# Mixture of experts: spreading the routing weights four rows at a time, and moving the residual sum to ACT and GpSimd

## The reference, cut to what matters

```python
t = t + _L1_ffn_ref(_ln_t(t), ...)          # 65536 tokens of 64 channels

def _L1_ffn_ref(x, router_w, router_b, expert_w, expert_b):
    B, N, D, C, E, K = (8, 4096, 64, 64, 8, 2)
    router_probs = jax.nn.softmax(x @ router_w + router_b, axis=-1)
    top_p, top_i = jax.lax.top_k(router_probs, K)
    top_p = top_p / jnp.sum(top_p, axis=-1, keepdims=True)
    expert_out = jnp.einsum('bnd,edc->bnec', x, expert_w) + expert_b
    gathered = jnp.take_along_axis(expert_out, top_i[..., None], axis=2)
    return jnp.einsum('bnk,bnkc->bnc', top_p, gathered)
```

## Time and profile before

| | |
|---|---|
| timed executions (three) | median 2308.48 us, 2306.16 to 2319.19 |
| profiled execution | 2298.41 us, span of the instructions 2296.6 us |
| PE / VectorE busy over the whole span | 1752.8 us (76%) / 1584.8 us (69%) |
| ACT / GpSimd busy over the whole span | 1142.8 us (50%) / 1168.2 us (51%) |
| the experts | first load of x at 1715.5 us, first spread at 1761.9, last store issued at 2292.6 |
| granted clock, mean over the span | 0.913 |

### The profile page before, as it was taken

How to read it: one execution, slowest core, us unless ns; L and a number is a source line. 1 busy time by engine, 2 the same in 40 slices (tenths; PEclk the granted TensorE clock), 3 DMA queues, 4 the chain that set the end, 5 groups by cost and what they waited for, 6 DMA issues and landing times. The chain is left out here.

```text
span 2296.6 us, 44402 instructions
## 1 busy us (share of the span) xinstructions
PE 1752.8 (76%) x11740; PEld 1164.1 (51%) x11740; DVE 1584.8 (69%) x5005; ACT 1142.8 (50%) x2610; POOL 1168.2 (51%) x1594
## 2 busy tenths in 40 slices
PE   5778748888646659838887737978746999999998
PEld 3444437778522238724444426877734444444443
DVE  6888704566757768838787730665664889889887
ACT  5898813333125549817676633333216545555541
POOL 5777604676857740026566520766765343444330
PEclk9999979999779989959999979999885999999999
DMA  3777547888633314958789746988764555555552
GB/s 115 204 193 190 156 137 240 273 297 284 209 117 93 95 51 82 191 179 242 233 252 267 217 115 179 311 276 272 260 193 144 155 157 158 155 158 160 153 140 68
DMA packets 475473, 423.19 MB, mean 184 GB/s; under 512 B 224690, under 2 KB 372402, under 8 KB 475314
## 3 DMA queue, kind: packets, MB, share of 16 engines
q1 hardware_dynamic: 402610, 303.87, 47.4%
q10 hardware_dynamic: 72704, 117.47, 15.2%
HBM read 236.68 MB, written 150.99 MB: 169 GB/s over the span
## 5 line engine op out<-in xcount | busy, mean ns | idle before, releaser
L699 PE MATMUL cp_pv<-cp_weight,cp_zt 64*128 64x320 f32 x2048 | 369.8, 469 | 103.4 <-ACT cp_zt L637 87.8
L257 POOL TENSOR_TENSOR cc_ln_rstd<-cc_ln_var,numbers 128x8 f32<-128x8 f32 x128 | 255.5, 1996 | 188.5 <-DVE cc_ln_var L248 179.6
L523 DVE SCALAR_TENSOR_TENSOR a_res<-cp_pv,cp_mask,cp_sig 128x64 f32<-128x64 f32 x1024 | 263.9, 322 | 123.9 <-ACT cp_sig L646 119.4
L1537 DVE TENSOR_TENSOR ex_xe<-ex_spread,ex_xd 128x512 f32<-128x512 f32 x512 | 322.6, 683 | 36.0 <-PE ex_spread L1779 35.8
L829 PE MATMUL cc_sum<-a_res,cc_bch 128*128 (+1 forms) x2048 | 297.9, 296 | 62.6 <-DMA cc_bch<-b_scratch 59.3
L919 ACT ACTIVATE cc_p<-cc_sum 128x512 f32 (+1 forms) x128 | 135.8, 1061 | 376.4 <-PE cc_sum L829 239.7
L829 PEld LDWEIGHTS cc_sum<-a_res,cc_bch 128*128 128x128 f32 x2048 | 269.8, 205 | 85.0 <-issue 76.1
L646 ACT ACTIVATE cp_sig<-cp_pv 128x384 f32<-128x384 f32 x512 | 249.7, 493 | 125.7 <-PE cp_pv L699 124.0
L699 PEld LDWEIGHTS cp_pv<-cp_weight,cp_zt 64*128 64x128 f32 x2048 | 184.3, 189 | 222.3 <-issue 193.7
L1796 PE MATMUL ex_po<-ex_xe,ex_expert 128*64 128x512 f32 x1024 | 267.8, 647 | 0.1
L1589 POOL TENSOR_TENSOR ex_rstd<-ex_var,numbers 128x8 f32<-128x8 f32 x64 | 104.7, 1636 | 270.4 <-DVE ex_var L1485 260.5
(11 more groups left out here) (186 smaller groups left out, 2976.4 us busy)
## 6 DMA issues: line engine op xcount, KB each, us to landing
cc_bch<-b_scratch SPq DMA_DIRECT2D x256, 256.0 KB, 3.9
gate_scratch<-cp_sig SPq DMA_DIRECT2D x128, 256.0 KB, 2.6
b_scratch<-cp_b_stage SPq DMA_DIRECT2D x128, 256.0 KB, 4.0
cc_g<-gate_scratch ACTq DMA_DIRECT2D x128, 256.0 KB, 4.5
after_conv<-cc_p ACTq DMA_DIRECT2D x128, 256.0 KB, 3.8
ex_xd<-ex_xt SPq DMA_DIRECT2D x256, 128.0 KB, 2.5
cp_x<-in_x SPq DMA_DIRECT2D x64, 256.0 KB, 3.3
cc_p<-in_x ACTq DMA_DIRECT2D x64, 256.0 KB, 3.6
```

The costliest lines, as they stand in the source:

```text
L257: pool.tensor_tensor(rstd[q][:], var[q][:], numbers[:, 0:1].to_broadcast([P, tiles]), ALU.pow).then_inc(scaled if shifts else known, 1)
L523: dve.scalar_tensor_tensor(a_res[:, h, :, row], bank[:, h, 3 * C:4 * C], mask_sb[:, h, row:row + 1], sig[u.mod(2)][:, 0, h, i, :], ALU.mul ...
L699: pe.matmul(pv[slot(u, i)][:, h, 0:COLS], zt[u.mod(2)][half, i * P:(i + 1) * P], weight[half, :], start=True, stop=True).then_inc(v_made, 1)
L1537: dve.tensor_tensor(xe[u.mod(2)][:, :, h, i * P:(i + 1) * P], pb[2 * (p % 2) + h][:].rearrange("p (e t) -> p e t", e=EP), xd[u.mod(8)][:, ...
```

## The change

- The spreads of a unit come in two groups instead of four. A group fills all four banks with 16 matmuls, of which four in a row use the four different groups of 32 rows (`FOURS`). It may start when all four blocks of the group before are done. Each bank has a semaphore of its own.
- VectorE's step: four blocks, half of the measuring, the choosing or the split, four blocks, the rest of the measuring, the choosing. Measuring is one unit further ahead.
- The sum with x leaves VectorE. ACT copies `tb` into the new tile `turned` (`take_turned`, first in its step), and GpSimd adds it to `rest` (`finish`, first in its step). The store comes a step later.
- PE's order in a step: experts half 1, flip, spread, experts half 2, rating, spread of the next unit, transposes of the output. Before: spread, flip, experts half 1, spread, experts half 2, spread, rating, spread, transposes.
- ACT normalises in two parts around `take`. The tiles of x are 8 instead of 4, those of the statistics 4 instead of 2, and the loop has one step more at each end.

The diff, cut to its core:

```diff
-        xs = [m.sb(f"x{q}", [P, H, R, C]) for q in range(4)]
+        xs = [m.sb(f"x{q}", [P, H, R, C]) for q in range(8)]
...
+        turned = [m.sb(f"turned{q}", [P, R * P]) for q in range(2)]
...
+        FOURS = [[(0, 0), (1, 1), (0, 2), (1, 3)], [(1, 0), (0, 1), (1, 2), (0, 3)]]
+        FIRST, LAST, HEAD, TAIL = -13, G + 2, 16, 16
...
 (SyncE)
-                    load(s + 12)
+                    load(s + 13)
                     double(s + 7)
-                    load_rest(s + 1)
+                    load_rest(s)
...
 (VectorE)
+                def scale_inputs(u, g, k):
+                    h, i = FOURS[g][k]
...
+                    dve.wait_ge(spread_made[k], u.n * 2 + g + 1)
                     dve.tensor_tensor(xe[u.mod(2)][:, :, h, i * P:(i + 1) * P],
-                                      pb[2 * (p % 2) + h][:].rearrange("p (e t) -> p e t", e=EP),
+                                      pb[k][:].rearrange("p (e t) -> p e t", e=EP),
...
-                    scale_inputs(s, 0, 0)
-                    scale_inputs(s, 0, 1)
-                    finish(s - 2)
-                    scale_inputs(s, 1, 0)
-                    scale_inputs(s, 1, 1)
-                    measure(s + 10)
+                    for k in range(4):
+                        scale_inputs(s, 0, k)
+                    measure(s + 11, 0)
                     if turn == 0:
                         choose(four, 0)
                     if turn == 1:
                         choose(four, 2)
                     if turn == 3:
                         split_shares(s + 1)
-                    scale_inputs(s, 2, 0)
-                    scale_inputs(s, 2, 1)
-                    scale_inputs(s, 3, 0)
-                    scale_inputs(s, 3, 1)
+                    for k in range(4):
+                        scale_inputs(s, 1, k)
+                    measure(s + 11, 1)
...
 (GpSimd)
+                def finish(u):
+                    if not u.real:
+                        return
+                    pool.wait_ge(turned_copied, u.n + 1)
+                    pool.wait_ge(rest_in[u.mod(4)], u.div(4) * 16 + 16)
+                    to = rest[u.mod(4)][:].rearrange("p h i c -> p i h c")
+                    pool.tensor_tensor(to, turned[u.mod(2)][:].rearrange("p (i h c) -> p i h c", i=R, h=H), to, ALU.add
+                                       ).then_inc(out_made, 1)
...
+                    finish(s - 2)
                     if turn == 1:
                         weigh(four, 1)
                     find_scales(s + 10)
...
 (ACT)
+                def take_turned(u):
...
+                    act.activation(turned[u.mod(2)][:], tb[:], ACT.Copy).then_inc(turned_copied, 1)
...
+                    take_turned(s - 2)
                     if turn == 3:
                         take_shares(s + 1)
+                    normalise(s + 9, 0)
                     take(s + 8)
-                    normalise(s + 9)
-                    store(s - 2)
                     if turn == 2:
                         weigh(s + 2)
+                    normalise(s + 9, 1)
                     take_outputs(s - 1)
+                    store(s - 3)
                     take_logits(s + 8)
...
 (TensorE)
-                    if p >= 2 or (u - 1).real:
-                        pe.wait_ge(xe_dve, u.n * DVE_BLOCKS + 2 * p - 2)
+                    if g or (u - 1).real:
+                        pe.wait_ge(xe_made, (2 * u.n + g) * R)
...
                     for e in range(EP):
-                        for h in range(H):
-                            q = (p + h) % R
-                            ins = pe.matmul(pb[2 * (p % 2) + h][:, e * P:(e + 1) * P],
-                                            select[32 * q:32 * q + 32, h, e, :], rows[32 * q:32 * q + 32, :],
-                                            start=True, stop=True)
+                        for k, (h, i) in enumerate(FOURS[g]):
+                            ins = pe.matmul(pb[k][:, e * P:(e + 1) * P], select[32 * i:32 * i + 32, h, e, :],
+                                            rows[32 * i:32 * i + 32, :], start=True, stop=True)
                             if e == EP - 1:
-                                ins.then_inc(spread_b if h else spread_a, 1)
+                                ins.then_inc(spread_made[k], 1)
...
-                    spread_out(s, 2)
+                    add_experts(s - 1, 0)
                     flip(s + 8)
-                    add_experts(s - 1, 0)
-                    spread_out(s, 3)
+                    spread_out(s, 1)
                     add_experts(s - 1, 1)
+                    rate(s + 8)
                     spread_out(s + 1, 0)
-                    rate(s + 8)
-                    spread_out(s + 1, 1)
                     turn_outputs(s - 1)
```

More of the change, by code:

```diff
@@ L1361, in experts @@
         yt = m.sb("yt", [P, R * P])
[L1362 to L1365 removed]
+        turned = [m.sb(f"turned{q}", [P, R * P]) for q in range(2)]
+        stats = [m.sb(f"stats{q}", [P, T, 3]) for q in range(4)]
+        var = [m.sb(f"var{q}", [P, T]) for q in range(4)]
+        rstd = [m.sb(f"rstd{q}", [P, T]) for q in range(4)]
+        lift = [m.sb(f"lift{q}", [P, T]) for q in range(4)]
         T4 = 4 * T
@@ L1406, in _ @@
                 dve.tensor_copy(router[:], pb[1][:, 0:H * E]).then_inc(weights_made, 1)
-        x_in = [m.sem(f"x_in{q}") for q in range(4)]
+        x_in = [m.sem(f"x_in{q}") for q in range(8)]
         rest_in = [m.sem(f"rest_in{q}") for q in range(4)]
```

100 lines of the change are left out of this document (46 added, 54 removed).

## The result

| | before | after |
|---|---|---|
| timed executions (four each, on one chip) | median 2307.32 us, 2304.51 to 2319.19 | median 2228.52 us, 2223.46 to 2237.77 |
| profiled execution, its span | 2298.41 us, 2296.6 | 2233.01 us, 2231.2 |
| granted clock, mean over the span | 0.913 | 0.924 |

The ratio is 0.9653 (95% interval 0.9611 to 0.9696): faster by 79 us. Forecast were 54.5 us. Three terms of the sum were too small: the pace at full clock, what the clock gives back, and the first units.

The account below looks back on a forecast made before the run. Neither PE nor VectorE alone bound it: each needs just under 30 of 31.67 us per four, the rest is hand-over. 33.4+15.1+5.2+2-1.2=54.5 us off the median of 2308.5 gave 2254.0 us, range 2240 to 2285.

Parts of the forecast that it names:

- Warm pace: Experts, 13 fours at full clock: 31.67 us per four falls to 29.1, saving 33.4 us.
- the rule: Spreads start at the later of PE's work done and VectorE's previous first block plus 2.63; 28.82 us per four.
- for the four semaphore updates a group and GpSimd's lateness I add 0.3: Allowance added to the pace of a four, giving 29.1 us.
- I let a third stay: Clock term, 13 fours: of 22.7 us lost to clock falls a third remains, 15.1 us come back.
- as often as now: Rival: PE still pauses and the clock falls as before, the 15 us don't come, 2269 us; chance 0.15.
- second rival: The clock falls as often as now, supported by the skill's page on PSUM cycling; 2269 us, chance 0.15.
- First units: Start of the experts, at half clock: 2 us saved.
- Last units: Last 11 units: 3.5 us from the first four, 0.24 for each of seven without flip or rating; 5.2 saved.
- End: End of the experts: copy and add in a row instead of one sum, 1.2 us longer.
- GpSimd's order: Add first in GpSimd's step; turn 1's masking loses its cover. Rival of GpSimd being late: 2280 us, chance 0.10.
- The add holds VectorE: Slower rival: GpSimd's add locks with VectorE's variance, 1.1 us in each B; about 2330 us at 35.5, chance 0.05.
- Two groups of rows: Rival: only two row groups run at once, spread group 0.55 us, 17 us lost, 2271 us; chance 0.13.

Follow-up runs that it names:

- e4_long_pause: Kernel after with two more VectorE reductions at the end of turn 0's step, lengthening PE's pause behind the flip; 2230.34 us in one execution.
- e6_extra_add: Kernel after with one more two-input GpSimd operation of 128x512 per unit, timed to meet VectorE's variance; 2270.34 us in one execution.
- e1_fours_only: Kernel after with the sum with x back on VectorE in mid-step, spreads still in fours; 2248.06 us, ratio 0.9752.
- e2_sum_only: Kernel before with only the sum with x moved to ACT and GpSimd; 2280.35 us, ratio 0.9895.
- v2_pool_order: v1_measure_placed with GpSimd masking ahead of the sum in turn 1, scales last and one unit earlier, ACT's shares ahead of `take`; 2208.14 us, ratio 0.9596.
- v1_measure_placed: Kernel after with measuring placed by turns (none in turn 1, more in turns 2 and 3), loads two steps earlier; 2245.15 us, ratio 0.9738.
- e7_two_row_groups: Kernel after with blocks dealt so that a group's 16 spread matmuls use two groups of 32 rows, not four; 2244.65 us in one execution.
- e8_pause_behind_rating: Kernel after with two more VectorE reductions in the middle of turn 1's step, lengthening PE's pause behind the rating; 2234.41 us in one execution.

## Why the prediction was wrong in size and right in kind

**Warm pace: 29.1 us per four forecast, 28.47 measured; 33.4 us forecast for 13, 41.6 measured.** The mechanism is the one described. From spread group to spread group (A from a unit's first to its second, B to the next unit's first; a unit is named by its turn), with the rule as it stood in the prediction:

| | A0 | B0 | A1 | B1 | A2 | B2 | A3 | B3 | sum |
|---|---|---|---|---|---|---|---|---|---|
| forecast | 3.38 | 3.20 | 4.21 | 3.75 | 3.90 | 3.20 | 3.98 | 3.20 | 28.82 |
| measured | 3.38 | 3.19 | 4.14 | 3.68 | 3.81 | 3.20 | 3.93 | 3.20 | 28.53 |

PE waits in the three places forecast, 0.69, 0.40 and 0.36 us instead of 0.83, 0.55 and 0.52, and nowhere else. The rule was 0.3 too high, most of it in the three intervals that VectorE sets, where the block follows a choosing step sooner (0.34 us behind its start, 1919.25 to 1919.59). The step that failed is the one behind it: "for the four semaphore updates a group and GpSimd's lateness I add 0.3". The 13 fours show no such cost: PE waits for VectorE's blocks alone, and VectorE for GpSimd once, 0.4 us. And the rule's own error was known to have that sign, since it gave 31.9 for a trace of 31.67. Both together are 0.63 us for a four, 8.2 us.

**Clock: 22.7 us lost before, 15.1 forecast back, 22.7 came back.** "I let a third stay": none stayed. The forecast argued from the pauses, that they do not vanish, and gave too little to the other half of its own sentence, that rating, spread and transposes no longer lie with the long pause. Pauses of 0.69 us remain in the kernel after and no fall in the 13 fours, and one of 1.47 us at the same place brought none (e4_long_pause), though one of 2.35 us did (e6_extra_add). What makes the clock fall stays open, so that all of it came back is in part luck. The rival "as often as now" is refuted; it would have been right for the spreads alone, where a pause of 0.90 us is left in the light stretch.

The Trainium skill ("TensorE: Matmul & The Clock Gate", Part 1, psum-queue depth-cycling) describes a kernel in which PE idles briefly and often between groups of matmuls that cycle through PSUM banks, and in which the clock swings between its levels. The prediction took it as speaking for its second rival. In the trace of after PE idles so as well, in 38 waits for VectorE's blocks, and the clock doesn't swing: 1.00 over 370 us.

**First units: 2 forecast, 6.8 measured.** The first spread comes 2.3 us sooner behind the stage's start, and the first output copy 4.5 us sooner behind the spread. The clock rises 10.3 us behind the first spread instead of 15.1. The table above says where it is from: the spreads with the new order of work bring it (51.1 and 14.0 us in e1_fours_only), the sum brings none of it (53.8 and 17.6 in e2_sum_only). With two groups of rows the first copy comes 1.7 to 2.3 us later than in its neighbours. The term "at half clock: 2" gave no working; it left out that the clock would rise sooner.

**Last units: 5.2 forecast, 4.5 measured.** That these are close is luck. The first four gave 5.7 us (32.8 before, 27.1 after) where 3.5 were forecast. The seven units behind it lost 1.2 (43.4 before, 44.6 after) where 1.7 were to be gained, although units without flip and rating take 6.2 us, near the 6.12 forecast: VectorE's wait of 0.90 us for the masking makes a pause of 1.90 us ahead of PE's spread at 2181.41, and a fall of the clock follows. v2_pool_order leaves 69.1 us in place of 71.8. **End: -1.2 forecast, -0.8 measured.**

**The sum.** 41.6 + 22.7 + 6.8 + 4.5 - 0.8 = 74.8 against 54.5. Of the 20.3 missing, 8.2 are the pace, 7.6 the clock, 4.8 the first units; the last units and the end take 0.3 off. The medians differ by 78.8; the last 4 lie within what the stages ahead of the experts vary by, and are not explained.

**The range failed at its low end.** Its best case took a clock that never falls, which came true, but with 28.8 for the pace and 2 for the first units: 66. With 28.5 and 6.8 it is some 75. All terms were set on the careful side, so the end that was meant to hold the best of everything held the best of one.

**GpSimd's order: right.** "No cover is left" for the masking: 0.02 us were (1922.44 against 1922.46), and 0.96 us of waiting came when the cover was taken (v1_measure_placed). As a rival it was wrong for the 13 fours of this kernel, right for its last units and for the next edit.

**The add holds VectorE: mechanism right, place right, price too high.** Forecast was that only the shares' add of turn 2 meets the variance. GpSimd in that step:

```profile
1903.86 1.28 POOL L1619 TENSOR_TENSOR ex_shares<-ex_first,ex_second 128x512 f32<-128x512 f32 x1
```

VectorE:

```profile
1904.50 0.66 DVE L1488 TENSOR_SCALAR ex_var<-ex_stats 128x8 f32<-128x8 f32 x1
```

Both end about 1905.15; 13 of the 64 variances are such, and PE is the bound there. Where nearly every unit has the hold (e6_extra_add), the rival's price was 1.1 us in each B and 35.5 for a four with the clock. Measured were 29.9 in the best fours and 31.99 in the mean, so the rival wouldn't have made the kernel slower than before. In a four without a fall four holds of 0.85 us and one of 0.80 make 4.2, and the four is 2.4 longer; the rest lies where PE has work left.

**Two groups of rows: rival refuted, price right.** 17 us were named for it; e7_two_row_groups has a stage 19.3 us longer than the kernel after. The Trainium skill ("TensorE: Matmul & The Clock Gate", Part 3) gives 3.07 times for four row groups of matmuls with 512 columns; by that the group would have been near 0.40, an estimate from that page, and the trace has 0.33, so that loss doesn't show at this size.

## What to carry to other kernels

Where two engines hand work to and fro, write the time from hand-over to hand-over as a recurrence with durations and latencies of the trace; it placed every pause of the kernel after, and it missed by 2.3 us for a four, falls of the clock among them, where a third engine, GpSimd, was left out of it. Treat the order of PE's work as something that the clock can depend on: moving light work away from a pause that can't be avoided went here with 2 falls instead of 11 (and with a shorter pause), but heavy work on either side carried a pause of 1.47 us and not always one of 2.35. So look at the granted clock again after each change of order. When work moves to GpSimd, look at the trace for what of VectorE starts while it runs, and for what GpSimd now does later.

## What was new of the hardware

- Matmuls of 32 rows and 128 columns, four groups of rows at a time, take no longer than two at a time: 16 in 0.33 us, against 8 in 0.33. With two groups of rows 16 take 0.55. The order within the sixteen hardly matters (0.35).
- A two-input operation of 128x512 on GpSimd holds not only VectorE's TENSOR_SCALAR on eight elements (0.17 to 1.24 us), which the earlier trace rows had shown, but a TENSOR_TENSOR with both inputs in SBUF as well (0.42 to 1.22). The blocks of `xe`, with one input in PSUM, aren't held: 672 to 693 ns in all 512 records of e6_extra_add, of which 105 start while such an operation runs. The Trainium skill ("GPSIMD Engine Reference", section 1) names VectorE's instructions with two SBUF inputs among those that contend with GpSimd; the trace agrees, and gives the price.
- A pause between rating and spread was followed by a fall of the clock in 4 of 12 cases (1.06 us, e8_pause_behind_rating), 6 of 12 (0.96, v1_measure_placed) and 11 of 12 (0.90, e1_fours_only). A pause between flip and spread was so in 0 of 13 (1.47, e4_long_pause) and 7 of 13 (2.35, e6_extra_add). The kernels differ in more than the pause, and its length doesn't order them.
